# A two-stage sequence kernel: g turned by TensorE, one row layout in DRAM, fewer and larger DMAs, stores issued by ScalarE

## The chip, the cores and the metric

One core of a Trainium2 chip runs the whole program. The metric is device microseconds of one launch. The times are the median of several launches; the profile is one further launch with the hardware profiler on. TensorE is PE, VectorE is DVE, ScalarE is ACT, GpSimd is POOL and SyncE is SP. SP computes nothing here, it issues nearly all DMAs. In the rows, PEld is TensorE's weight load, and SPq and ACTq are the instruction queues of SP and ACT.

## The reference

`x` has 64 batches of 128 channels by 2048 times, in fp32. Two residual steps follow each other:

```python
x = x + einsum('bct,bcd->bdt', x, weights[condition])      # 16 possible 128x128 matrices, one is picked per batch
K = 2 * einsum('hn,hnl->hl', Ct, exp(dtA * l)).real         # one long filter of 2048 taps per channel, 64 complex modes
y = irfft(rfft(x, 4096) * rfft(K, 4096))[:2048] + x * D     # causal convolution of each channel in time, plus a gain
x = x + y * (time < length[batch])
```

The first step mixes channels inside a batch, the second works along time inside a channel. So everything has to change its layout once between them.

## The kernel before

**Mixing.** For batch n, SP loads `x_f` (128 channels by 2048 times, 1 MB). POOL makes `w_buf` (the picked matrix plus the identity), PE multiplies in four quarters of 512 columns, and the result is copied out of PSUM into `stage` with time reversed inside blocks of 128. `store_half` (L376 to L388) sends each half of a batch to DRAM in two DMAs: 48 channels to `u_wide` (192 KB, L385), 80 channels to `u_full` (320 KB, L387).

**Convolving.** It runs in 64 slots. Slots 0 to 11 are wide: four channels, batches 0 to 31. The other half of the batches of these channels comes back later as 12 more wide slots; the other 40 slots are narrow: two channels, all 64 batches. From slot 12 on the order is three narrow slots, one wide, twelve times, and then four narrow ones. A slot always handles 1 MB: `u_row`, 128 partitions of 2048 floats. `load_u` brings it as four DMAs of 256 KB in a wide slot (L395) and as two of 512 KB in a narrow one (L400), PE transposes it (L747), ACT and DVE split it into two fp16 parts in `u_t`. PE then computes the inputs to the states with `gt_sb` (L765, once per slot), advances the states over seven chunks (L781), and adds the taps (L803, L809) and the states' part (L822) to the output. ACT copies the output to `o_sb` (L942), DVE overlays the masked part (L1226), and SP stores it: `store_out`, four DMAs per slot.

**The tables.** POOL and ACT make `g_sb` for each pair of channels (called a tab; a wide slot has two, a narrow one has one). `transpose_g` turns it into `gt_sb` with two transposing DMAs per tab (L435). In slots 0 to 11 SP also keeps `g_sb` in DRAM (L439) for the later wide slots, which load it back (L419) and turn it again. The Toeplitz table comes from DRAM, one DMA of 256 KB in runs of 512 bytes per tab (L408).

**The order.** Step c of the program works on slots side by side: the taps and outputs of slot c-1, the states of slot c, the transposes of slot c+1. Each is cut into eight parts, k = 0 to 7. Batches 0 to 34 are mixed ahead of slot 0. Batches 35 to 63 are mixed in quarters inside slots 0 to 9 (`MIXED`, `LATER` = 10), with PSUM banks 6 and 7 taken in turn. SP's instructions stand in one fixed order and each waits for the one before. In a mixing slot (`mixing_slot`) SP issues 3 loads of x, 12 stores to `u_wide` and `u_full`, 4 loads of `u_row`, 2 Toeplitz loads, 4 transposing DMAs, 2 stores of g and 4 output stores: 31 DMAs. In a narrow slot it is 9. The narrow slots need both halves of the batches, so slot 12's load waits until all 64 batches have landed in DRAM.

**Two forms of output store.** In `store_out` (L442 to L455) the two kinds of slot write with different access patterns. The form of a wide slot is this, and its DRAM side begins with a dimension of four:

```python
dst = bass.AP(out.tensor, SLOTS[s].part * NBW * H * T + (SLOTS[s].first + v) * T,
              [[UNIT, 4], [H * T, NBW], [1, UNIT]])          # L447, store at L449
```

A narrow slot stores a channel in two DMAs of 64 batches by 1024 times:

```python
dst = bass.AP(out.tensor, (SLOTS[s].first + v // 2) * T + j * HALF, [[H * T, NB], [1, HALF]])   # L453, store at L454
```

Both move 256 KB each, four to a slot.

## Time and profile before

| | us |
|---|---|
| median of three launches | 1270.88 (1268.12 to 1271.56) |
| the profiled launch | 1265.78 |
| its span, first to last instruction | 1263.5 |
| PE busy | 1054.1 (83%) |
| DVE busy | 756.5 (60%) |
| POOL busy | 623.3 (49%) |
| ACT busy | 560.3 (44%) |

The launch falls into three stretches. Up to about 229 us batches 0 to 34 are mixed. Up to about 577 us slots 0 to 9 run together with the mixing of the rest. Then only slots are left. The page gives each engine's busy time over the whole, so the shares above mix three different limits. In the rows further down "DMA share" is the busy share of the 16 DMA engines in a stretch, and in the pictures of forty digits each digit is that share in tenths in a fortieth of the stretch.

### The profile page before, as it was taken

Reading aid. Unit: us, or ns where it says so; the run is one execution under the profiler, and the core shown is the slowest. Engines: PE = TensorE matmul, PEld = TensorE weight load, DVE = VectorE, ACT = ScalarE, POOL = GpSimd, SP = SyncE. Lnnn points to the kernel's source line nnn. Section 1 sums busy time; section 2 is a strip of 40 time slices with the busy share of each in tenths; the row PEclk is TensorE's granted clock in tenths of the full one; section 3 lists DMA queues with packets and bytes.
Section 4 is the critical chain, followed back from the end, with each engine's and each line's share of the span. In section 5 each row is a group of like instructions: output and inputs, shape, how many; then the busy total and the mean of one; then the engine's idle time right before and its main releaser. Section 6 shows DMA issues by size and latency. Waiting matters only on the chain.

```text
span 1263.5 us, 33041 instructions
## 1 busy us (share of the span) xinstructions
PE 1054.1 (83%) x12718; PEld 803.1 (64%) x12718; DVE 756.5 (60%) x1744; ACT 560.3 (44%) x1251; POOL 623.3 (49%) x1396
## 2 busy tenths in 40 slices
PE   8767774777767666785889999999999999999998
PEld 5223342454545444455768888888888878888886
DVE  4989710444334234333567777777777777777775
ACT  3533342333223223323345655655555555555554
POOL 3101427652344442223545757667568558657650
PEclk9988896889878878888999999999999999999999
DMA  9999999999998999998999999999899999999996
GB/s 344 393 340 398 401 353 306 264 307 271 272 264 250 265 246 254 248 245 204 167 209 258 256 210 249 254 227 249 208 272 248 214 260 256 221 249 249 199 243 155
DMA packets 238476, 330.91 MB, mean 262 GB/s; under 512 B 110242, under 2 KB 155682, under 8 KB 230130
## 3 DMA queue, kind: packets, MB, share of 16 engines
q1 hardware_dynamic: 238002, 328.35, 97.9%
q8 instruction: 103, 1.69, 0.6%
q0 software_dynamic: 160, 0.20, 0.2%
q14 instruction: 51, 0.42, 0.1%
q10 hardware_dynamic: 160, 0.26, 0.1%
HBM read 164.96 MB, written 140.71 MB: 242 GB/s over the span
## 4 chain that ended last, share of the span: by engine, by line
PE 53%; DMA 21%; SPq 19%; issue 4%; DVE 2%; ACT 2%; ACTq 0%
PE bank L803 10%; PE bank L822 10%; PE bank L765 8%; DMA u_row<-u_wide 7%; PE bank L747 7%; DMA u_row<-u_full 7%; SPq L435 6%; DMA u_full<-stage 5%; PE bank L781 5%; PE bank L713 5%; PE bank L726 4%; PE bank L809 4%; SPq L385 3%; SPq L387 2%; SPq L449 2%
## 5 line engine op out<-in xcount | busy, mean ns | idle before, releaser
L747 PE MATMUL bank<-ident,u_row 128*128 128x128 f32 x1024 | 287.0, 284 | 138.9 <-DMA u_row<-u_wide 120.2
L803 PE MATMUL bank<-toep,u_t 128*128 128x192 f16 (+1 forms) x3072 | 351.2, 223 | 0.3 <-issue 0.3
L603 POOL TENSOR_TENSOR g_sb<-g_x,g_sb 128x128 f16<-128x128 f32 x256 | 115.3, 484 | 348.5 <-ACT g_sb L891 348.5
L747 PEld LDWEIGHTS bank<-ident,u_row 128*128 128x128 f32 x1024 | 147.1, 145 | 158.9 <-DMA u_row<-u_wide 108.5
L803 PEld LDWEIGHTS bank<-toep,u_t 128*128 128x128 f16 x3072 | 237.0, 100 | 15.3 <-issue 3.9
L1204 DVE SCALAR_TENSOR_TENSOR u_t<-bank,u_t 128x512 f16<-128x512 f32 x256 | 176.3, 689 | 111.1 <-ACT u_t L920 110.0
L809 PE MATMUL bank<-toep,x_t 128*128 128x64 f16 x2048 | 193.2, 195 | 2.0 <-issue 2.0
L822 PE MATMUL bank<-g_sb,st_full 128*128 128x256 f16 x960 | 192.4, 274 | 0.2 <-issue 0.2
L920 ACT ACTIVATE u_t<-bank 128x512 f16<-128x512 f32 x256 | 151.6, 593 | 72.9 <-PE bank L747 72.3
L713 PE MATMUL bank<-x_f,w_buf 128*128 128x512 f32 x280 | 138.0, 644 | 45.6 <-issue 30.7
L765 PE MATMUL bank<-u_t,gt_sb 128*128 128x224 f16 (+1 forms) x1056 | 157.4, 302 | 9.0 <-issue 9.0
L809 PEld LDWEIGHTS bank<-toep,x_t 128*128 128x128 f16 x2048 | 161.6, 100 | 2.6 <-issue 2.2
L935 ACT ACTIVATE st_full<-bank 128x128 f16<-128x128 f32 x280 | 77.5, 277 | 174.4 <-PE bank L781 133.2
L942 ACT ACTIVATE o_sb<-bank 128x512 f32<-128x512 f32 x256 | 152.8, 597 | 4.0 <-PE bank L822 4.0
L619 POOL TENSOR_TENSOR w_buf<-w_f,ident 128x128 f32<-128x128 f32 x64 | 34.3, 538 | 222.9 <-PE bank L713 116.2
L765 PEld LDWEIGHTS bank<-u_t,gt_sb 128*128 128x128 f16 x1056 | 102.2, 98 | 54.8 <-issue 17.1
L713 PEld LDWEIGHTS bank<-x_f,w_buf 128*128 128x128 f32 x280 | 55.3, 205 | 123.1 <-issue 104.9
L726 PE MATMUL bank<-x_f,w_buf 128*128 128x512 f32 x232 | 130.9, 676 | 0.0
L1226 DVE COPY_PREDICATED o_sb<-mask,u_row 128x512 f32<-128x512 uint8 x160 | 123.5, 772 | 11.4 <-issue 11.3
L595 POOL TENSOR_TENSOR g_x<-g_x,g_y 128x128 f32<-128x128 f32 x256 | 127.3, 529 | 5.0
L610 POOL TENSOR_TENSOR lam_sb<-eyes,lam_v 128x128 f16<-128x128 f16 x256 | 118.9, 495 | 19.3 <-PE bank L781 19.3
L1209 DVE TENSOR_TENSOR st_full<-bank,st_full 128x128 f16<-128x128 f32 x280 | 81.7, 292 | 74.3 <-ACT st_full L935 71.2
(138 smaller groups left out, 1519.7 us busy)
## 6 DMA issues: line engine op xcount, KB each, us to landing
x_f<-in_x SPq DMA_DIRECT2D x64, 1024.0 KB, 10.5
out<-o_sb SPq DMA_DIRECT2D x254, 256.0 KB
u_full<-stage SPq DMA_DIRECT2D x128, 320.0 KB, 8.9
u_row<-u_full SPq DMA_DIRECT2D x80, 512.0 KB, 6.3
u_wide<-stage SPq DMA_DIRECT2D x128, 192.0 KB, 6.4
u_row<-u_wide SPq DMA_DIRECT2D x96, 256.0 KB, 8.7
toep<-k_scratch SPq DMA_DIRECT2D x88, 256.0 KB, 7.0
g_scratch<-g_sb SPq DMA_DIRECT2D x24, 256.0 KB, 4.5
```

The source lines that it names most:

```text
L595: pool.tensor_tensor(out=g_x[r][:, h, part], in0=g_x[r][:, h, part], in1=g_y[:, h, part], op=SUB)\
L713: last = pe.matmul(bank[:, 4 * (n % 2) + k, :], w_buf[n % WS][:, :], x_f[X_AT[n]][:, k * 512:(k + 1) * 512], start=True, stop=True)
L726: pe.matmul(bank[:, 6 + k % 2, :], w_buf[n % WS][:, :], x_f[X_AT[n]][:, k * 512:(k + 1) * 512], start=True, stop=True).then_inc(s_mq, 1)
L747: ins = pe.transpose(bank[:, u_bank(s, q), k % 4 * P:(k % 4 + 1) * P], ap(u_row[b], (h * groups(s) + g) * Q + tb * P, [[1, P]]), ident[:, :])
L765: last = pe.matmul(to, gt_sb[GT_AT[t]][:, hh, a, 1 - tb, :], ap(u_t[s % 3], u_at(s, h, tb, b, 0), [[1, cols]]), start=(m == 0 and fresh), ...
L803: pe.matmul(bank[:, y, col + tb * P + NM:col + Q], ap(u_t[s % 3], u_at(s, h, tb, a, gr), [[1, P]]), tp[:, hh, b, NM:Q - tb * P], start=fir ...
L809: pe.matmul(bank[:, y, col + tb * P:col + tb * P + NM], ap(x_t[s % 2], x_at(s, h, tb, gr), [[1, P]]), tp[:, hh, b, 0:NM], start=False, sto ...
L822: last = pe.matmul(bank[:, y, col:col + Q], ap(state_tile(s), st_at(s, h, a) + gr * P, [[1, P]]), g_sb[t % GS][:, hh, b, :], start=False, ...
L920: act.activation(u_t[s % 3][:, q, 0, :], bank[:, u_bank(s, q), :], ACT.Copy, scale=US).then_inc(s_uh, 1)
L942: act.activation(o_sb[o][:, v % 2, :], bank[:, 2 + v % 2, :], ACT.Copy, scale=1.0 / (US * KS))\
L1204: dve.scalar_tensor_tensor(out=t[:, q, 1, :], in0=bank[:, u_bank(s, q), :], scalar=US, in1=t[:, q, 0, :], op0=MUL, op1=SUB).then_inc(s_ul, 1)
L1226: dve.copy_predicated(o_sb[2 * (s % 2) + v // 2][:, v % 2, :].rearrange("p (b t) -> p b t", t=P), where.rearrange("p (b t) -> p b t", t=P) ...
```

## The change

It does five things.

1. `u_wide` and `u_full` become one tensor `u_dram` with 128 rows of 512 times for each channel and half of the batches. A half batch is stored in one DMA of 512 KB. Each slot loads `u_row` in two DMAs of 512 KB. All slots work with the same layout: a narrow slot is now four units of 32 batches by one channel.
2. `gt_sb` of slots 0 to 11 is made by PE: four matmuls against a swapped identity (`swap`) give half a tab in PSUM bank 6 or 7, and ACT or DVE copies it out. Mixing quarters and these halves form one list (`UNITS`); the halves of slot c+1 stand at k = 4 to 7 of step c. `g_sb` and `gt_sb` are stored in DRAM (`store_g`, two DMAs of 512 KB per slot) and the 12 later wide slots load both. The 40 narrow slots keep the transposing DMAs. A buffer of `gt_sb` can be written again only when its store has landed (`stored_g`).
3. Two Toeplitz tables that lie side by side are loaded in one DMA.
4. `store_out` uses one form for all slots, the one with the leading dimension of four. The output stores of slots 0 to 8 are issued by ACT, except for slot 8's last one; the very last slot's are shared between SP and ACT.
5. Six buffers of `x_f` are used up to batch 35 instead of 31 (`X_AT`).

The core of the diff:

```diff
-QUARTERS = {2: (1, 1, 1, 1, 1, 1, 1, 1), 3: (2, 1, 2, 1, 2, 1, 2, 1)}
+QUARTERS = {2: (1, 1, 1, 1, 1, 1, 1, 1), 3: (2, 2, 2, 2, 1, 1, 1, 1)}
-X_AT = [n % XS if n < NBW else n % (XS // 2) for n in range(NB)]
+X_AT = [n % XS if n <= FIRST else n % (XS // 2) for n in range(NB)]
...
+        def unit_copy(eng, u):
+            unit, half = UNITS[u], bank[:, 6 + u % 2, :]
+            eng.wait_ge(s_mq, u + 1)
...
+            s, last = SLOT_OF[unit.of], before(GT_AT, unit.of)
+            if last is not None:
+                eng.wait_ge(s_st, 7 * SLOT_OF[last] + 1)
+                stored_g(eng, last)
...
+        def store_out(eng, s, v):
+            o = 2 * (s % 2) + v // 2
+            eng.wait_ge(s_ov, 4 * s + v + 1)
+            dst = bass.AP(out.tensor, batches(s, v) * NBW * H * T + channel(s, v) * T, [[UNIT, 4], [H * T, NBW], [1, UNIT]])
+            eng.dma_start(dst, o_sb[o][:, v % 2, :]).then_inc(s_store[o], 16)
...
-                dst = bass.AP(u_wide, ((n // NBW * 4 + 2 * j) * NBW + n % NBW) * UNIT,
-                              [[2 * P * UNIT, H1], [NBW * UNIT, 2], [1, UNIT]])
-                sp.dma_start(dst, stage[b][0:H1, :].rearrange("p (a t) -> p a t", t=UNIT)).then_inc(s_us[b], 16)
-                dst = bass.AP(u_full, (j * NB + n) * HALF, [[P * HALF, H - H1], [1, HALF]])
-                sp.dma_start(dst, stage[b][H1:H, :]).then_inc(s_us[b], 16)
+                dst = bass.AP(u_dram, (n // NBW * P + 2 * j * NBW + n % NBW) * UNIT, [[2 * TILE, H], [NBW * UNIT, 2], [1, UNIT]])
+                sp.dma_start(dst, stage[b][:, :].rearrange("p (a t) -> p a t", t=UNIT)).then_inc(s_us[b], 16)
...
+                if last is not None:
+                    sp.wait_ge(s_ov, 4 * last + 2 * p + 2)
+                step = (channel(s, 1) - channel(s, 0)) * 2 + batches(s, 1) - batches(s, 0)
+                src = bass.AP(u_dram, (channel(s, 2 * p) * 2 + batches(s, 2 * p)) * TILE, [[UNIT, P], [step * TILE, 2], [1, UNIT]])
...
-                if n == FIRST - 2:
-                    transpose_g(0)
...
             def mixing_slot(c):
                 for k in range(8):
                     if k == 0:
                         if c > 0:
                             load_toeplitz(c)
-                        if has(c - 2):
-                            store_out(c - 2, 3)
-                        load_u(c + 1, 3)
-                    if k == 3:
-                        if c == 0:
-                            sp.wait_ge(s_kd, 80)
-                            load_toeplitz(c)
-                        transpose_g(c + 1)
-                    if k in (3, 5, 7):
-                        if has(c - 1):
-                            store_out(c - 1, k // 2 - 1)
-                        load_u(c + 2, k // 2 - 1)
+                        load_u(c + 1, 1)
+                    if k == 1:
+                        store_g(c)
+                    if k == 3 and c == 0:
+                        sp.wait_ge(s_kd, 80)
+                        load_toeplitz(c)
+                    if k == 5:
+                        load_u(c + 2, 0)
...
+                    for k in range(4):
+                        last = pe.matmul(to[:, k * P:(k + 1) * P], g_sb[of % GS][:, part, k // 2, k % 2 * P:(k % 2 + 1) * P],
+                                         swap[:, :, :].rearrange("p a m -> p (a m)"), start=True, stop=True)
...
             def out_evac(s, v):
...
+                if s < LATER - 1 and v > 0:
+                    store_out(act, s, v - 1)
+                if 0 < s < LATER - 1 and v == 0:
+                    store_out(act, s - 1, 3)
```

## Rows read from the trace of the kernel before

**Rows 1.** Busy time by stretch: engines, clock, DMA share, rate.
```profile
core 0: us, PE busy (x) PEld busy (x) DVE busy (x) ACT busy (x) POOL busy (x), PEclk, DMA share, GB/s
0.00:229.00 229.00, 163.66 (x616) 76.58 (x617) 133.76 (x327) 85.90 (x94) 70.11 (x181) 0.89 0.99 360
229.00:577.00 348.00, 249.56 (x2303) 168.15 (x2302) 133.57 (x278) 105.83 (x241) 136.82 (x348) 0.85 0.96 260
577.00:616.00 39.00, 27.22 (x434) 24.57 (x432) 19.36 (x44) 14.29 (x37) 12.42 (x29) 0.95 0.95 191
616.00:1209.00 593.00, 564.07 (x8641) 492.88 (x8640) 433.70 (x1008) 327.99 (x816) 390.05 (x812) 0.99 1.02 237
1209.00:1264.00 55.00, 49.58 (x732) 40.94 (x730) 36.08 (x89) 26.24 (x66) 13.88 (x28) 1.00 0.78 182
```

**Rows 2.** Timeline, the one L765 group of some slots: start, us, what.
```profile
229.35 2.46 PE L765 MATMUL bank<-u_t,gt_sb 128*128 128x224 f16 x24
...
287.32 2.46 PE L765 MATMUL bank<-u_t,gt_sb 128*128 128x224 f16 x24
...
576.85 1.40 PE L765 MATMUL bank<-u_t,gt_sb 128*128 128x224 f16 x8
...
615.94 2.43 PE L765 MATMUL bank<-u_t,gt_sb 128*128 128x448 f16 x12
...
631.64 2.82 PE L765 MATMUL bank<-u_t,gt_sb 128*128 128x448 f16 x12
...
709.87 1.31 PE L765 MATMUL bank<-u_t,gt_sb 128*128 128x224 f16 x12
...
721.96 2.43 PE L765 MATMUL bank<-u_t,gt_sb 128*128 128x448 f16 x12
...
1209.02 1.30 PE L765 MATMUL bank<-u_t,gt_sb 128*128 128x448 f16 x6
```

**Rows 3.** DMA packets from 100 to 150 us, in the first stretch.
```profile
DMA packets 5325, 20.07 MB, mean 401 GB/s; under 512 B 759, under 2 KB 759, under 8 KB 4083
```

**Rows 4.** DMA share and rate in forty slices, 608.5 to 612.5 us.
```profile
DMA  2239923222322222222222322322322322222329
GB/s 102 102 136 105 105 102 123 82 102 102 123 82 102 102 102 102 102 102 102 102 102 102 123 102 82 123 102 102 123 82 102 143 82 82 102 82 77 97 77 115
```

**Rows 5.** SP's queue around that, from 603 to 634 us.
```profile
603.40 1.28 SPq L400 DMA_DIRECT2D u_row<-u_full  x1
604.87 5.20 SPq L435 DMA_TRANSPOSE gt_sb<-g_sb  x2
610.12 1.62 SPq L449 DMA_DIRECT2D out<-o_sb  x2
...
617.61 1.21 SPq L400 DMA_DIRECT2D u_row<-u_full  x1
...
633.96 1.26 SPq L395 DMA_DIRECT2D u_row<-u_wide  x2
```

**Rows 6.** DMA share and rate, 626 to 630 us.
```profile
DMA  2223224302302122121234999999990000100000
GB/s 82 102 102 123 82 102 164 123 41 123 164 41 123 82 123 123 82 123 51 46 72 85 379 259 271 274 185 75 69 23 0 0 0 0 8 8 10 10 8 10
```

**Rows 7.** The same with only narrow slots' stores queued, 940 to 944 us.
```profile
DMA packets 1091, 1.38 MB, mean 344 GB/s; under 512 B 78, under 2 KB 676, under 8 KB 1090
```

**Rows 8.** Who waited for whom on PE, 229 to 577 us: total, times, longest.
```profile
PE bank L747 <- DMA u_row<-u_wide: 95.7, 25, 8.1
```

**Rows 9.** Around the first row load: SP's queue, and PE's wait.
```profile
189.72 6.95 SPq L435 DMA_TRANSPOSE gt_sb<-g_sb  x2
...
204.84 0.43 SPq L385 DMA_DIRECT2D u_wide<-stage  x1
...
217.00 1.30 PE L747 MATMUL bank<-ident,u_row 128*128 128x128 f32 x5 [17.16 <-DMA u_row<-u_wide]
```

**Rows 10.** The stores that ACT issues at the end.
```profile
1258.99 1.89 ACTq L362 DMA_DIRECT2D out<-o_sb  x2
```

More of the change, by code:

```diff
@@ L287, in stage_free @@
         def stage_free(eng, m):
-            wait(eng, s_us[STAGE_AT[m]], 32 * uses(STAGE_AT, m))
+            wait(eng, s_us[STAGE_AT[m]], 16 * uses(STAGE_AT, m))
         def stages_landed(eng, buffers, batches):
             for b in buffers:
-                eng.wait_ge(s_us[b], 32 * STAGE_AT[:2 * batches].count(b))
+                eng.wait_ge(s_us[b], 16 * STAGE_AT[:2 * batches].count(b))
         def mixing_over(eng):
-            eng.wait_ge(s_mq, 4 * (NB - FIRST))
-        def width(s):
-            return NBW if SLOTS[s].wide else NB
@@ new lines, in at, with new_state, channel, batches @@
+        def at(j):
+            return (j % 2 * 4 + j // 2) * NBW
+        def state(s, part, j):
+            return st_sb[s % 2][:, :, part, at(j):at(j) + NBW]
+        def new_state(j):
+            return ap(bank, at(j - 1), [[2 * P, 4], [1, NBW]])
+        def channel(s, v):
+            return SLOTS[s].first + (v if SLOTS[s].wide else v // 2)
+        def batches(s, v):
+            return SLOTS[s].part if SLOTS[s].wide else v % 2
+        def tab(s, v):
+            return (TABS[s][v // 2], v % 2) if SLOTS[s].wide else (TABS[s][0], v // 2)
@@ new lines, in load_toeplitz @@
+            def load_toeplitz(s):
+                t0, n = TABS[s][0], len(TABS[s])
+                together = n == 2 and TOEP_AT[t0] % 4 < 3 and TOEP_AT[t0 + 1] == TOEP_AT[t0] + 1
+                for t in [t0] if together else TABS[s]:
+                    for r in range(t, t + 1 + together):
+                        last = before(TOEP_AT, r)
+                        if last is not None:
+                            sp.wait_ge(s_out, 4 * (SLOT_OF[last] + 1))
+                    b, rows_ = TOEP_AT[t], 4 * (1 + together)
+                    src = bass.AP(k_dram, PAIR_OF[t] * (4 * KROW), [[1, P], [KROW, rows_], [1, Q]])
+                    to = ap((toep_now, toep_later)[b // 4], b % 4 * 4 * Q, [[Q, rows_], [1, Q]])
+                    sp.dma_start(to, src).then_inc(s_t[b], 16)
@@ new lines, in load_gt, with transpose_g @@
+                    sp.dma_start(gt_sb[b].rearrange("p h a b m -> p (h a b m)"), gt_dram[PAIR_OF[t], :, :]).then_inc(s_gt[b], 16)
+            def transpose_g(s):
+                t = TABS[s][0]
+                b, last = GT_AT[t], before(GT_AT, t)
+                if last is not None:
+                    sp.wait_ge(s_st, 7 * SLOT_OF[last] + 1)
+                    if SLOT_OF[last] < WIDE:
+                        stored_g(sp, last)
+                sp.sem_inc(s_go, 1)
+                sp.wait_ge(s_g, 4 * (MADE_NO[t] + 1))
+                sp.sem_inc(s_go, 1)
+                for lo in (0, NM):
+                    sp.dma_start(gt_sb[b][:, :, :, :, lo:lo + NM].rearrange("p h a b m -> p (h a b) m"),
+                                 g_sb[t % GS][NM - lo:P - lo, :, :, :].rearrange("p h a t -> p (h a t)"),
+                                 transpose=True).then_inc(s_gt[b], 16)
@@ L827, in states_part @@
                     last.then_inc(s_out, 1)
-            pe.wait_ge(s_ev, 2 * FIRST)
+            for u in range(PROLOGUE - 2):
+                unit(u)
             for k in range(8):
                 transpose_u(0, k)
-            for k in range(4):
-                mix(FIRST, k)
+            for u in range(PROLOGUE - 2, PROLOGUE):
+                unit(u)
             for k in range(8, 16):
@@ L854, in slot @@
                         between(2 * k + 1)
[L855 to L856 removed]
+                    for u in UNITS_AT[c][k]:
+                        unit(u)
                     if has(c) and k >= 2:
@@ L925, in fold_toeplitz @@
                     b = TOEP_AT[t]
-                    act.wait_ge(s_t[b], 16 * (uses(TOEP_AT, t) + 1))
+                    if landed_with(t) == t:
+                        act.wait_ge(s_t[b], 16 * (sum(landed_with(r) == r and TOEP_AT[r] == b for r in range(t)) + 1))
                     act.activation(toep[b][0:NM, :, :, 0:NM].rearrange("p h a t -> p (h a) t"),
@@ L975, in _ @@
             slots(slot)
-            for v in range(2):
-                store_last(act, 1, v)
+            for v in (1, 3):
+                store_out(act, NSL - 1, v)
         @block.vector
@@ L1224, in overlay @@
                 dve.memset(pad[0:1, at:at + 1], 0.0)
-                where = mask_w[:, SLOTS[s].part, :] if SLOTS[s].wide else mask[:, UNIT * (v % 2):UNIT * (v % 2 + 1)]
+                where = mask[:, batches(s, v), :]
                 dve.copy_predicated(o_sb[2 * (s % 2) + v // 2][:, v % 2, :].rearrange("p (b t) -> p b t", t=P),
@@ L1230, in _ @@
             make_lambda(0)
+            for u in range(1, PROLOGUE - 2, 2):
+                unit_evac(u)
             u_lo(0, 0)
             u_lo(0, 1)
-            mix_evac(FIRST, 1)
-            mix_evac(FIRST, 3)
+            unit_evac(PROLOGUE - 1)
             u_lo(0, 2)
```

431 lines of the change are left out of this document (199 added, 232 removed).

## The prediction

> **What bounds the kernel now.** I read the stretches first [rows 1], then the slots' starts [rows 2], then what PE waits for, and last SP's queue beside the DMA rate. Three stretches have three limits. Up to 229 us the DMA engines carry 360 GB/s on average and 401 in the middle of it [rows 1, 3]: that is what 16 engines give here, 25.1 GB/s each, so this stretch goes at the pace of transfers. From slot 0 to slot 10 (229.35 to 576.85, 347.5 us) PE is busy for 250 us and waits 95.7 us for `u_row` loads [rows 1, 2, 8]; transfers rule again, but at 260 GB/s. From slot 12 to slot 60 (615.94 to 1209.02, 593.1 us) PE is busy 95% of the time and sets the pace: a wide slot takes 12.09 us and a narrow one 11.35 when nothing is late [rows 1, 2], and a group of three narrow and one wide took 593.1 / 12 = 49.4 against 3 x 11.35 + 12.09 = 46.1.
>
> Why 260 GB/s when 401 is to be had? Look at the digits around 610 us [rows 4]: the share of busy engines is 2 to 3 tenths for most of 4 us and the rate stands at 102 GB/s. That is a quarter of the engines at full rate, 25.5 GB/s each. In SP's queue ahead of that stand output stores of wide slots (the L449 form), and no `u_wide` load is near [rows 5]. So I read: a store whose DRAM side begins with a dimension of four runs on four engines only, 0.262 MB / 102 GB/s = 2.57 us each. With stores of the narrow form queued the rate is 344 GB/s [rows 7], so those spread over all 16. The Trainium skill has the rule behind it (DMA: Bandwidth & Descriptors, section Why a DMA increments its semaphore by 16 and not by 1): the number of engines is the largest up to 16 that divides the slowest dimensions of both sides, here 4 and 128. By it every store of the new kernel runs on four engines, and the trace agrees for the form that it shows.
>
> **The change, the stores.** It gives the L449 form to all slots. Four stores of 256 KB then put 256 KB on each of four engines per slot, where a narrow slot's now put 64 KB on all sixteen. Work of the fullest engines in a narrow slot, in KB each: stores 256, rows 1 MB / 16 = 64, Toeplitz 16, turning 16: 352 KB. At 25.5 GB/s that is 14.1 us, more than PE's 11.35. The trace already holds this mix: from 603 to 634 us SP's cycle is one narrow slot's loads, two transposing DMAs and four wide-form stores. The two cycles took 14.21 and 16.35 us, and slot 12 to slot 13 took 15.70 on PE [rows 2, 5]. The longer one shows what is added: SP stands 5.20 us on two transposing DMAs, and at 628 us the rate falls to nothing for a moment behind the drain [rows 5, 6]. I take 15.8 us, near the two longer readings, since each narrow slot keeps its two transposing DMAs; the bounds are 14.2 and 16.4.
>
> A wide slot behind slot 12 has stores 256, rows 64, Toeplitz 32, g 32 and gt 32: 416 KB, 16.7 us, without transposing DMAs of its own; today it would be the same without its four of those. A group becomes 3 x 15.8 + 16.7 = 64.1 us, and 12 groups 769 instead of 593: +176. The bounds are 14.1 per narrow slot, giving 59.0 and +115, and 16.4 with 18.5 for the wide one (the same 10% over its bytes), giving 67.7 and +219. Behind slot 60 two slots still have loads and lose about 4 us each, and the last slot's stores need up to two more stores' time: +12 (0 to +20).
>
> **The change, the mixing slots.** Their stores have the four-engine form already. In a step with three batches the fullest engines carry 256 + (3 + 3 + 1 + 0.5 + 0.5 + 0.5) MB / 16 = 800 KB, 32.1 us, and with two batches 672 KB, 27.0. Steps 2 to 9 (slot 2 to slot 10, 289.5 us [rows 2]) hold six of the first and two of the second: 247 us, so 43 us are lost between, 5.3 per step. Each step has two pairs of transposing DMAs, and one pair held SP for 5.20 us [rows 5]. The pairs go; the extra `gt` store takes their bytes' place. I give each step 1.5 us back to other gaps: 259 us, a gain of 31, and 8 for steps 0 and 1, which lose the same pairs but hold fewer stores. Sum -39. It can't go under PE's 250 us of work plus 40 half tabs; four half tabs are 16 short matmuls per step, and I count 1 us, so the bound is -65 with some idle time left. On the other side it can be 0: 31 DMAs per step become about 19, of which four move to ACT, but SP wasn't short of time by itself, the engines were.
>
> Where new waits lie: a `u_row` pair is now loaded only after two overlays, at k = 5 instead of 3 and 5, with three eighths of a step (12 us at 32) for 512 KB to land; the copy of a half tab at k = 4 waits on ACT or DVE for the store of the half tabs of the slot before, issued at k = 1, and behind it stand the mixing copies and the states of that engine, for which PE waits. Both have about 12 us, so I price them at nothing and keep 0 as the bound above. ACT's DMA issue costs 1.89 / 2 = 0.95 us at most including gaps [rows 10]; 35 of them are 33 us of an engine that is busy 106 of 348 [rows 1]. What hides them is that slack.
>
> Here a rule speaks against me and one against the change. Advanced Engine Details and Errata, section X-Bar Transpose (TRN2), of the Trainium skill says that transposing DMAs are as fast as regular ones; then 128 KB each would be 1.3 us per step at 401 GB/s and the gain of 39 would be some 10 instead. SP's 5.20 us and the empty slices say otherwise. And DMA: Bandwidth & Descriptors, section Issuing engines are not separate DMA queues, of the skill says that a second issuing engine adds no bandwidth, only issue time; by that the move to ACT brings nothing, and I count nothing.
>
> **The change, the rest.** Ahead of slot 0 SP stands from 189.72 to 204.84 on transposing DMAs and the g stores before it issues the last row's stores and then the first row load, and PE waits 17.16 us for it until 217.00 [rows 9]. Without them that load can go about 14 us earlier; PE has batches 33 and 34 loaded earlier by the six buffers, and turns half tabs meanwhile. I take -13. Bounds -17 (all of the wait) and 0 (packets of 2 KB instead of 4 KB could cost; but the stores of [rows 4] are 2 KB packets at 25.5 GB/s per engine, no slower than the 25.1 of [rows 3]). Slots 10 and 11: their stores were of the wide form before, only the transposing pairs of slot 11 go: -3 (0 to -6). PE's narrow slots keep their columns and counts; the access patterns get one dimension more, at nothing. POOL's few memsets too.
>
> **How the numbers follow.** Against the profiled launch: 1265.8 - 13 - 39 - 3 + 176 + 12 = 1398.8. The median of the launches is 5 us (0.4%) above the profiled one, so 1404. A measurement of this kernel can tell about 0.3% (4 us) from no change.
>
> *Forecast, 57%:* 1404. Its own range is 1345 (the short cycles) to 1455.
>
> *Rival 1, the stores are hidden better, 12%.* Engines run ahead while PE waits, groups take 59.0 and the mixing goes at PE's bound: 1404 - 61 - 26 = 1317.
>
> *Rival 2, the mixing gains nothing, 12%.* The `u_row` pairs or the landed g stores are late in each step. For: two overlays and one issue instead of finer pieces. Against: 12 us each. 1404 + 39 = 1443.
>
> *Rival 3, everything in series, 9%.* SP's ring is held by the four full engines, so rows and turning can't run beside stores: 4 x 2.57 + 1.6 MB / 401 GB/s + 5.2 = 19.5 us per narrow slot, and 10.3 + 2.6 MB / 401 = 16.8 for a wide one: 75.3 per group, 904 for twelve, +135: 1539. Against it is the cycle of 14.21.
>
> *Rival 4, on the other side, 9%.* The four engines belong to something else than the form of the store (the place in the queue, the tile), and the narrow slots' stores stay spread. Then the change only removes transposing DMAs and issues, and SP's shorter wide slots let PE run at 46.1 per group: 1265.8 - 13 - 39 - 3 - 39 + 5 = 1177. The point from which it decides: a group stays at 49.4 if the fullest engine carries no more than 1229 KB, that is 195 KB per slot for stores, so from six engines on the stores cost nothing. The Trainium skill's rule for kernel authors on the same DMA page, to merge into transfers of 1 MB or more, points this way too: 256 KB stores merged into 512 KB loads.
>
> One in a hundred is left for no change, where gains and losses cancel. So faster 0.09, same 0.01, slower 0.90. The range of 1315 to 1480 leaves out rivals 3 and 4.
>
> **What the profile would show.** Right: the starts of L765 lie 15 to 17 us apart from slot 12 on; PE's busy share there falls from 95% to about 75%, with `u_row` named as what it waits for; the rate sits at about 102 GB/s with digits of 2 for long runs; slot 0 starts near 216 and slot 10 near 525. Wrong at once: a rate of 300 GB/s and intervals of 11.4 us from slot 12 on (rival 4), or slot 10 still at 560 or later (rival 2).

## The result and the profile after

| | before | after |
|---|---|---|
| median | 1271.2 us | 1371.95 us (1368.88 to 1373.14, four launches) |
| span of the profiled launch | 1263.5 | 1369.2 |
| ratio | 1 | 1.079 (1.0765 to 1.082) |

The change makes the kernel 101 us slower. The forecast was 1404, with a range of 1315 to 1480, so the sign and the range hold and the middle is 32 us too high.

The busy times by stretch, cut at the same slots as [rows 1] (slot 0, slot 10, slot 12, slot 60):

```profile
core 0: us, PE busy (x) PEld busy (x) DVE busy (x) ACT busy (x) POOL busy (x), PEclk, DMA share, GB/s
0.00:209.00 209.00, 158.45 (x633) 73.77 (x634) 132.92 (x315) 86.93 (x96) 67.45 (x167) 0.93 1.01 395
209.00:505.00 296.00, 238.42 (x2459) 165.64 (x2458) 144.72 (x297) 117.50 (x260) 133.18 (x327) 0.91 0.88 304
505.00:544.00 39.00, 28.43 (x454) 26.39 (x453) 20.19 (x47) 15.76 (x39) 18.67 (x41) 0.87 0.69 203
544.00:1292.00 748.00, 610.18 (x8640) 521.05 (x8639) 430.97 (x1009) 331.08 (x818) 355.72 (x821) 0.94 0.89 187
1292.00:1370.00 78.00, 51.49 (x730) 41.87 (x728) 35.55 (x88) 25.59 (x64) 10.53 (x24) 0.87 0.62 136
```

The starts behind these cuts, from the timeline. L793 is what L765 was in [rows 2], here at slots 0, 2, 10, 12, 13 and 60:

```profile
209.70 1.50 PE L793 MATMUL bank<-u_t,gt_sb 128*128 128x224 f16 x14
...
267.77 1.41 PE L793 MATMUL bank<-u_t,gt_sb 128*128 128x224 f16 x13
...
505.24 0.93 PE L793 MATMUL bank<-u_t,gt_sb 128*128 128x224 f16 x8
...
543.64 1.68 PE L793 MATMUL bank<-u_t,gt_sb 128*128 128x448 f16 x8
...
560.39 1.46 PE L793 MATMUL bank<-u_t,gt_sb 128*128 128x448 f16 x4
...
1291.89 1.31 PE L793 MATMUL bank<-u_t,gt_sb 128*128 128x448 f16 x6 [0.42 <-DMA gt_sb<-g_sb]
```

Subtracting the starts of [rows 2] gives the balance by stretch:

| stretch | before | after | change | forecast |
|---|---|---|---|---|
| start to slot 0 | 229.35 | 209.70 | -19.7 | -13 |
| slot 0 to 10 | 347.5 | 295.5 | -52.0 | -39 |
| slot 10 to 12 | 39.1 | 38.4 | -0.7 | -3 |
| slot 12 to 60 | 593.1 | 748.25 | +155.2 | +176 |
| slot 60 to the end | 54.5 | 77.3 | +22.8 | +12 |
| sum | | | +105.6 | +133 |

So the part up to slot 10 gains 72 us, and the slots behind slot 12 lose 178. Behind slot 12 a group of four slots takes 748.25 / 12 = 62.35 us instead of 49.4. PE does the same matmuls (8640 against 8641), but its busy share falls from 95% to 610 / 748 = 82%. What it waits for there, in order of size (total, times, longest):

```profile
PE bank L770 <- DMA u_row<-u_scratch: 112.8, 56, 4.9
PE bank L810 <- issue: 6.9, 2, 3.7
```

Of the 138 us in which PE stands, 113 are waits for rows, and the next line is 6.9.

The page's summary of the chain that ended last says the same: transfers first, then PE's own work, and SP's queue third with 6%:

```profile
DMA 49%; PE 34%; SPq 6%; DVE 4%; issue 3%; ACT 3%; DVEq 0%; ACTq 0%
```

SP's queue from 900 to 940 us shows three narrow slots. The row loads stand 14.29 and 15.36 us apart, the pair of transposing DMAs takes SP 5.4 and 6.2 us:

```profile
906.87 1.20 SPq L426 DMA_DIRECT2D u_row<-u_scratch  x1
908.27 5.39 SPq L486 DMA_TRANSPOSE gt_later<-g_sb  x2
913.71 1.88 SPq L395 DMA_DIRECT2D out<-o_sb  x2
921.16 1.54 SPq L426 DMA_DIRECT2D u_row<-u_scratch  x1
922.90 6.20 SPq L486 DMA_TRANSPOSE gt_later<-g_sb  x2
...
936.52 1.27 SPq L426 DMA_DIRECT2D u_row<-u_scratch  x1
```

Four microseconds of the DMA engines inside that, from 922 us on. In the first twelve slices two tenths of the engines work for the most part, at 82 to 159 GB/s, as in [rows 4]: stores drain. From the 21st slice on, with the next load and the transposing DMAs in flight, the rate stands between 312 and 476 for twelve slices:

```profile
DMA  4222322232223999443399899999998944798997
GB/s 159 82 82 102 143 82 82 103 123 102 82 102 123 184 225 184 143 123 102 123 405 343 312 394 476 374 333 435 471 389 328 348 156 151 195 381 207 215 184 189
```

In the mixing slots PE's wait for rows fell from the 95.7 us of [rows 8] to 50.3, and the new wait for the stored half tabs appears four times on DVE:

```profile
PE bank L770 <- DMA u_row<-u_scratch: 50.3, 14, 8.6
...
DVE gt_sb L1220 <- DMA gt_scratch<-gt_sb: 17.2, 4, 6.5
```

At the end the last compute instruction stops at 1351.0 us and 18 us follow in which only stores run. From 1356 to 1369 us they stay at 101 GB/s, with digits of 2, until they run out in the last four slices:

```profile
1350.28 0.72 DVE L1255 COPY_PREDICATED o_sb<-mask,u_row 128x512 f32<-128x512 uint8 x1 [0.70 <-issue]
...
DMA  2222222222222222222222222222222222221000
GB/s 101 101 101 101 101 101 101 113 88 113 101 101 101 101 101 113 101 101 101 101 101 101 101 101 101 101 101 113 101 101 101 101 101 101 101 113 69 19 0 0
```

### The profile page after: what moved, and what is told of

The parts are those of the page before. It is cut to its first block, busy times and chain, and to the rows that moved or that the text cites. A ratio compares the mean times of both kernels' runs of the same rounds, so it can differ in the third digit from the quotient of the medians.

```text
span 1369.2 us, 33160 instructions
## 1 busy us (share of the span) xinstructions
PE 1087.0 (79%) x12910; PEld 828.7 (61%) x12910; DVE 764.3 (56%) x1754; ACT 576.9 (42%) x1275; POOL 585.5 (43%) x1377
## 4 chain that ended last, share of the span: by engine, by line
DMA 49%; PE 34%; SPq 6%; DVE 4%; issue 3%; ACT 3%; DVEq 0%; ACTq 0%
DMA u_row<-u_scratch 33%; DMA u_scratch<-stage 9%; PE bank L831 6%; PE bank L849 6%; PE bank L770 5%; PE bank L748 5%; PE bank L793 4%; DMA gt_scratch<-gt_sb 4%; PE bank L736 3%; PE bank L837 2%; PE bank L810 2%; SPq L395 2%; DVE o_sb L1255 2%; DVE u_t L1233 2%; SPq L462 2%
## 5 line engine op out<-in xcount | busy, mean ns | idle before, releaser
L849 PE MATMUL bank<-g_sb,st_sb 128*128 128x256 f16 x1536 | 326.6, 286 | 4.6 <-issue 4.6
L961 ACT ACTIVATE st_sb<-bank 128x128 f16<-128x128 f32 x448 | 123.9, 277 | 310.1 <-PE bank L810 220.7
L1238 DVE TENSOR_TENSOR st_sb<-bank,st_sb 128x128 f16<-128x128 f32 x448 | 130.2, 291 | 173.6 <-ACT st_sb L961 167.8
L831 PE MATMUL bank<-toep,u_t 128*128 128x192 f16 (+1 forms) x1752 | 208.2, 226 | 0.0
L1255 DVE COPY_PREDICATED o_sb<-mask,u_row 128x512 f32<-128x512 uint8 x256 | 195.9, 766 | 16.0 <-issue 15.9
L849 PEld LDWEIGHTS bank<-g_sb,st_sb 128*128 128x128 f16 x1536 | 155.7, 102 | 13.1 <-issue 4.8
L831 PE MATMUL bank<-toep_later,u_t 128*128 128x192 f16 (+1 forms) x1320 | 154.8, 226 | 2.6 <-issue 2.6
L810 PE MATMUL bank<-st_sb,lam_sb 128*128 128x32 f16 (+1 forms) x3168 | 147.0, 184 | 9.4 <-issue 6.9
L810 PEld LDWEIGHTS bank<-st_sb,lam_sb 128*128 128x128 f16 x3168 | 132.3, 97 | 35.7 <-issue 21.3
L831 PEld LDWEIGHTS bank<-toep,u_t 128*128 128x128 f16 x1752 | 139.5, 103 | 11.3 <-issue 3.9
```

Of the source, the lines that this page charges most:

```text
L810: last = pe.matmul(ap(bank, v * 2 * P + at(j), [[2 * P, n], [1, NBW]]), lam_sb[t % LS][:, h, a, :, :].rearrange("p k m -> p (k m)"), st_sb ...
L831: pe.matmul(bank[:, y, col + tb * P + NM:col + Q], ap(u_t[s % 3], v * 2 * UNIT + a * UNIT + tb * 2 * P + gr * P, [[1, P]]), tp[:, h, b, NM ...
L849: last = pe.matmul(bank[:, y, col:col + Q], st_sb[s % 2][:, v, a, gr * P:(gr + 1) * P], g_sb[t % GS][:, h, b, :], start=False, stop=(m == ...
L1238: dve.tensor_tensor(out=state(s, 1, j), in0=new_state(j), in1=state(s, 0, j), op=SUB).then_inc(s_stl, 1)
L1255: dve.copy_predicated(o_sb[2 * (s % 2) + v // 2][:, v % 2, :].rearrange("p (b t) -> p b t", t=P), where.rearrange("p (b t) -> p b t", t=P) ...
```

## The experiments

The theory is that the store with a leading dimension of four runs on four engines, and that this alone makes the loss. The main rivals are that the stores aren't the cause (rival 4), that their addresses are and not the number of engines, that SP's queue is (transposing DMAs, order), and that the move to ACT matters.

### The number of engines: sixteen, eight, and sixteen for narrow slots only

`k16_all` and `k8_all` keep the number and size of all stores and their place in the program. They change only the addresses in `out`, so that the leading dimension is 16 or 8; the output lands in another order, so these kernels serve for timing alone. `k16_narrow` does it for narrow slots alone.

```diff
-            dst = bass.AP(out.tensor, batches(s, v) * NBW * H * T + channel(s, v) * T, [[UNIT, 4], [H * T, NBW], [1, UNIT]])
+            k = 16                  # k8_all: 8; k16_narrow: 4 if SLOTS[s].wide else 16
+            row = 4 * NSL * UNIT
+            dst = bass.AP(out.tensor, (4 * s + v) * UNIT, [[row, k], [k * row, P // k], [1, UNIT]])
```

> The changed kernel with one edit: the DRAM side of each output store begins with a dimension of 16 instead of 4; same 256 KB, same runs of 2 KB, same waits. The output lands in another order, so it isn't the reference's. Theory (stores of the old form fill four engines, and these set the pace): from slot 12 on PE sets the pace again, a group of three narrow slots and a wide one takes 46 to 48 us instead of 62.4 (-180), the mixing steps fall from 296 to about 265, the end shrinks by 20: 1372 - 180 - 30 - 20 = about 1140, and no run of slices at 102 GB/s is left. Rival (the loss comes from the pair loads of u_row, from runs of 2 KB or from the new waits, not from the stores): 1372, unchanged.

> As k16_all, but the store's leading dimension is 8. Theory: the fullest engines carry 4 x 128 + 448 = 960 KB per group, 38.6 us, which is under PE's 46.1, so the time is within 20 us of k16_all (1140 to 1160): the number of engines costs nothing above the point where PE sets the pace. Rival (the cost goes with the share of engines left idle): half way between 1140 and 1372, about 1255.

> As k16_all, but only for narrow slots; the 24 wide slots keep a leading dimension of 4. Theory: the mixing steps stay at 296 us, groups take about 48 us, so 1372 - 173 - 20 = about 1180, which is what the fourth rival of the prediction gave (1177). If wide slots behind slot 12 slow their neighbours too, up to 1200. Rival (not the stores): 1372.

Measured, with the ratio to the kernel before:

| | us | ratio | slot 0 to 10 | group behind slot 12 |
|---|---|---|---|---|
| changed kernel | 1372.0 | 1.079 (1.0765 to 1.082) | 295.5 | 62.4 |
| `k16_all` | 1112.7 | 0.876 (0.869 to 0.883) | 253.7 | 46.5 |
| `k8_all` | 1132.9 | 0.891 (0.884 to 0.898) | 261.7 | 47.5 |
| `k16_narrow` | 1177.1 | 0.925 (0.918 to 0.932) | 294.6 | 48.3 |

The two stretches of `k16_all`, slot 0 to 10 and slot 12 to 60, then slot 12 to 60 of `k8_all`:

```profile
209.50:463.20 253.70, 230.65 (x2459) 161.28 (x2458) 146.34 (x297) 116.39 (x259) 137.21 (x326) 0.95 1.01 355
498.40:1056.90 558.50, 555.61 (x8642) 490.20 (x8641) 432.44 (x1009) 327.65 (x817) 397.22 (x816) 1.00 0.97 252
```

```profile
506.30:1076.00 569.70, 558.04 (x8642) 491.45 (x8641) 432.44 (x1009) 327.90 (x817) 393.07 (x816) 1.00 1.01 247
```

The same number of stores of the same size, issued at the same places, cost 259 us less. PE is busy for 555.6 of 558.5 us: it sets the pace again, with next to nothing late. Eight engines are nearly as good as sixteen, about as the break-even of rival 4 has it (from six engines on the stores cost nothing in a group). They are not quite free: the intervals of the two ratios don't overlap, and a group takes 1.0 us more. `k16_narrow` makes rival 4's condition true, and its 1177.1 stands beside the 1177 that was worked out for that rival. The agreement of the totals hides terms that were off and cancelled, as said further down.

The number of engines shows in the last 4 us of these launches too, where stores are all that is left. With a leading dimension of four the rate was 101 GB/s and the digits 2 (above). With eight (`k8_all`, 1128.4 to 1132.4 us) the commonest rate is 205, with digits around 5:

```profile
DMA  6454556355545735391465445543310000000000
GB/s 225 164 205 164 205 205 205 123 205 225 205 164 225 205 123 164 123 205 61 164 246 184 164 164 225 205 164 123 143 41 20 0 0 0 0 0 0 0 0 0
```

With sixteen (`k16_all`, 1106.7 to 1110.7 us) the digits are mostly 8 and 9, and the rate comes up to some 400, in one slice to 492:

```profile
DMA  0035969498979999889999987988632000000000
GB/s 0 0 82 164 225 123 287 82 205 225 328 287 369 410 389 287 287 348 492 369 389 369 369 205 205 287 307 307 246 143 82 0 0 0 0 0 0 0 0 0
```

### The same form in the kernel before

Is the form also what held the kernel before in its mixing slots? `before_k16` is the kernel before with only the stores of wide slots at a leading dimension of 16. They go to another tensor, so that part of the output, 96 of the 256 stores (not half, as the expectation has it), is missing.

```diff
-                    dst = bass.AP(out.tensor, SLOTS[s].part * NBW * H * T + (SLOTS[s].first + v) * T,
-                                  [[UNIT, 4], [H * T, NBW], [1, UNIT]])
+                    row = 4 * NSL * UNIT
+                    dst = bass.AP(spill, (4 * s + v) * UNIT, [[row, 16], [16 * row, P // 16], [1, UNIT]])
```

> The kernel before with one edit: the stores of its 24 wide slots (96 of 256) go with a leading dimension of 16 to another DRAM tensor, so half of the output is missing. Theory: slots 0 to 9 were held by four engines as well; 348 us become about 300, slots 10 to 15 lose some 25 us of waits, later groups 1 us each: about 1190. Rival (in the mixing slots of before SP's issues and transposing DMAs were the limit, not the four engines): the mixing stays near 340 and only slots 10 to 15 gain, 1240.

Measured 1180.35 us, 0.929 (0.921 to 0.937). Slot 0 to 10 took 290.8 us instead of 347.5, a group 47.5 instead of 49.4:

```profile
230.80:521.60 290.80, 233.65 (x2301) 158.83 (x2300) 134.08 (x277) 105.47 (x241) 141.02 (x345) 0.91 1.04 310
```

So the kernel before carried the same fault in 24 of its 64 slots, for 89 us (1269.45 in this comparison). Its mixing slots took 290.8 with the transposing DMAs and everything else as it was.

### A form that leaves the output where it is: each store cut by time

`split4` stores what a pair of 256 KB stores held in four DMAs of 128 KB, one for each quarter of the time. Each has 32 partitions on the SBUF side and a leading dimension of 32 batches on the DRAM side.

```diff
+            if v % 2 == 0:
+                return
...
-            dst = bass.AP(out.tensor, batches(s, v) * NBW * H * T + channel(s, v) * T, [[UNIT, 4], [H * T, NBW], [1, UNIT]])
-            eng.dma_start(dst, o_sb[o][:, v % 2, :]).then_inc(s_store[o], 16)
+            first = batches(s, v - 1) * NBW * H * T + channel(s, v - 1) * T
+            step = batches(s, v) * NBW * H * T + channel(s, v) * T - first
+            for a in range(4):
+                dst = bass.AP(out.tensor, first + a * UNIT, [[H * T, NBW], [step, 2], [1, UNIT]])
+                eng.dma_start(dst, o_sb[o][a * NBW:(a + 1) * NBW, :, :]).then_inc(s_store[o], 16)
...
```

> The changed kernel, complete, in its own row order; only each pair of output stores of 256 KB becomes four stores of 128 KB, one per time quarter, 32 partitions each. Their DRAM side then begins with 32. The price is four DMA issues more per slot (13 instead of 9 in a narrow one, 0.6 us each: 8.0 + 2.4 = 10.4 us of SP in 11.35 of PE). Theory (four engines): near k16_all, 1115 to 1145, faster than both kernels. Rival (the permuted addresses of k16_all were easier on DRAM, or SP becomes the bound): 1200 or more, with PE waiting for row loads.

Measured 1128.49 us (1127.1 to 1134.7), 0.885 (0.881 to 0.889). That is faster than both kernels: 243 us under the changed one and 145 under the one before. Slot 0 to 10, slot 12 to 60, and the issues of the stores on SP (ns shortest/median/longest):

```profile
209.50:463.10 253.60, 228.43 (x2460) 160.21 (x2459) 149.10 (x297) 115.86 (x260) 137.65 (x327) 0.95 1.00 355
498.70:1071.40 572.70, 559.12 (x8643) 491.43 (x8642) 435.90 (x1009) 328.55 (x818) 392.87 (x816) 1.00 0.98 246
```

```profile
L400 SPq DMA_DIRECT2D out<-o_sb x440: 315/432/2440, 463.4 to 1121.5; - x147
```

There are twice as many store DMAs of half the size, and the median issue takes SP 432 ns. A group takes 47.7 us, close to the 47.5 of `k8_all` and 1.2 us over the 46.5 of `k16_all`; whether the issues cost that difference isn't shown.

`before_split4` makes the same cut in the wide stores of the kernel before, and nothing else:

```diff
+                    if v % 2 == 0:
+                        return
...
-                    dst = bass.AP(out.tensor, SLOTS[s].part * NBW * H * T + (SLOTS[s].first + v) * T,
-                                  [[UNIT, 4], [H * T, NBW], [1, UNIT]])
-                    sp.dma_start(dst, o_sb[o][:, v % 2, :]).then_inc(s_store[o], 16)
+                    for a in range(4):
+                        dst = bass.AP(out.tensor, SLOTS[s].part * NBW * H * T + (SLOTS[s].first + v - 1) * T + a * UNIT,
+                                      [[H * T, NBW], [T, 2], [1, UNIT]])
+                        sp.dma_start(dst, o_sb[o][a * NBW:(a + 1) * NBW, :, :]).then_inc(s_store[o], 16)
...
```

> The kernel before, complete, in which only the output stores of its 24 wide slots are cut: each pair of 256 KB becomes four of 128 KB whose DRAM side begins with 32. It asks how much of the kernel before was held by four engines, with the true addresses. Theory: like before_k16, 1175 to 1200, though SP gets four issues more in steps where it already had 31 (0.45 us each, so up to 15 us more in the mixing steps). Rival (SP's issues were the limit of the mixing steps): 1240 or more.

Measured 1174.68 us, 0.922 (0.9185 to 0.9255):

```profile
229.60:520.80 291.20, 239.18 (x2302) 160.78 (x2301) 134.33 (x277) 104.91 (x241) 137.55 (x336) 0.90 1.04 307
```

Now the change can be taken apart. The kernel before is at 1273.6 in this comparison; spreading its wide stores gives 1174.7 (-99), all the rest of the change on top of that gives 1128.5 (-46), and the four-engine form on every store puts 243 back. Of the 46, 38 lie between slot 0 and 10 (291.2 to 253.6) and 20 ahead of slot 0 (229.60 to 209.50); behind slot 12 it gives back 11 (562.0 to 572.7).

### The move to ACT

`sp_stores` gives the stores of slots 0 to 8 back to SP, at the places that they had before.

```diff
+                        if has(c - 2):
+                            store_out(sp, c - 2, 3)
...
+                    if k in (3, 5, 7) and has(c - 1):
+                        store_out(sp, c - 1, k // 2 - 1)
...
-                if s < LATER - 1 and v > 0:
-                    store_out(act, s, v - 1)
-                if 0 < s < LATER - 1 and v == 0:
-                    store_out(act, s - 1, 3)
```

> The changed kernel with the output stores of slots 0 to 8 issued by SP, as in the kernel before; form with the leading dimension of 4 kept. The prediction counted nothing for the move to ScalarE: 1372, within 10 us. Rival: stores that fill four engines hold up SP's queue and everything behind it, which ACT's own queue avoids: the mixing steps go from 296 back towards 330, so 1390 to 1410.

Measured 1379.5 us, 1.083 (1.076 to 1.091), against the changed kernel's 1.079 (1.0765 to 1.082). The intervals overlap, so this run can't tell the two apart. Its profile has 303.0 us between slot 0 and 10 against 295.5, and one store issue that held SP for 6.7 us:

```profile
L395 SPq DMA_DIRECT2D out<-o_sb x36: 542/554/6696, 245.2 to 512.0; - x36
```

A gain of up to some 8 us from ACT is therefore possible beside four-engine stores, and not shown. The same step in a kernel with spread stores is `batch_major_sp`, below.

### The turning in the narrow slots

`no_turn` is the changed kernel whose narrow slots load the same number of bytes into `gt_sb` in two plain DMAs instead of two transposing ones. They come from DRAM and are the table of another pair, so the narrow slots leave out the turning and don't give the reference's result.

```diff
+                stored_g(sp, 0)
...
-                    sp.dma_start(gt_sb[b][:, :, :, :, lo:lo + NM].rearrange("p h a b m -> p (h a b) m"),
-                                 g_sb[t % GS][NM - lo:P - lo, :, :, :].rearrange("p h a t -> p (h a t)"),
-                                 transpose=True).then_inc(s_gt[b], 16)
+                    sp.dma_start(gt_sb[b][lo:lo + NM, :, :, :, :].rearrange("p h a b m -> p (h a b m)"),
+                                 gt_dram[0, lo:lo + NM, :]).then_inc(s_gt[b], 16)
```

> The changed kernel, but the 40 narrow slots load gt with two plain DMAs of 128 KB from the table of pair 0 instead of turning their own g, so their numbers are wrong. It tests the part of the sum that was put on turning, 1.7 us per narrow slot over the bytes of the fullest engines. Theory: groups fall from 62.4 to about 59 us, 1372 - 41 = 1331. Rival (the fullest engines work without a gap anyway): groups stay at 62, 1372.

Measured 1348.6 us, 1.057 (1.051 to 1.063), where 1331 was expected. Slot 12 to 60:

```profile
551.40:1275.00 723.60, 604.69 (x8642) 517.96 (x8641) 433.46 (x1009) 330.94 (x817) 357.51 (x819) 0.94 0.57 193
```

A group takes 723.6 / 12 = 60.3 us, 2.05 less than the 62.35 of the changed kernel: 0.7 us per narrow slot. The profiled launch is the slowest of the four, 5 us over the median, which is at most 0.14 us more per narrow slot. The forecast put 1.7. And 60.3 is close to the 59.0 that the bytes of the fullest engines alone give.

### The other way to spread the stores: rows in another order

`batch_major` puts the batch ahead of the quarter in the order of the 128 rows. A store then has a leading dimension of 32, stays one DMA of 256 KB and writes the very addresses that the changed kernel's store writes; only the order of the dimensions differs. The states of one chunk stand four elements apart in `st_sb` and in PSUM.

```diff
-            return (j % 2 * 4 + j // 2) * NBW
+            return j % 2 * P + j // 2
...
-            return st_sb[s % 2][:, :, part, at(j):at(j) + NBW]
+            return ap(st_sb[s % 2], part * 2 * P + at(j), [[4 * P, 4], [4, NBW]])
...
-            dst = bass.AP(out.tensor, batches(s, v) * NBW * H * T + channel(s, v) * T, [[UNIT, 4], [H * T, NBW], [1, UNIT]])
+            dst = bass.AP(out.tensor, batches(s, v) * NBW * H * T + channel(s, v) * T, [[H * T, NBW], [UNIT, 4], [1, UNIT]])
```

> The changed kernel, complete, with the rows of a tile ordered by batch first and time quarter second. The DRAM side of an output store then begins with a dimension of 32, and the half batches are stored in runs of 4 KB. The price is 32 idle columns more in each L765 matmul (about 0.3 us per slot, 20 us in all) and state copies with a step of four. Theory (four engines): 1113 + 20 = about 1130, faster than both kernels. Rival (the permuted addresses of k16_all were easier on DRAM than the true ones with their pitch of 1 MB): 1200 or more.

Measured 1261.4 us, 0.991 (0.987 to 0.994): 111 us under the changed kernel, and some 130 over what was expected. Slot 0 to 10 took 250.5, which is as good as `k16_all`. With the same addresses, number and size of stores as in the changed kernel, which took 295.5, this leaves the order of the dimensions and speaks against the addresses as the cause (the half batches are stored in runs of 4 KB here instead of 2 KB). But a group took 58.0 us, with PE's busy time at 660 us where `k16_all` has 556, and its clock at 1.00:

```profile
496.10:1192.00 695.90, 659.70 (x8643) 521.70 (x8642) 483.54 (x1008) 381.29 (x815) 370.12 (x814) 1.00 0.72 201
```

The groups by line show what grew. Busy us and mean ns of the two copies of a state, in the changed kernel first:

```profile
L961 ACT ACTIVATE st_sb<-bank 128x128 f16<-128x128 f32 x448 | 123.9, 277 | 310.1 <-PE bank L810 220.7 <-PE bank L793 89.4
L1238 DVE TENSOR_TENSOR st_sb<-bank,st_sb 128x128 f16<-128x128 f32 x448 | 130.2, 291 | 173.6 <-ACT st_sb L961 167.8
```

```profile
L959 ACT ACTIVATE st_sb<-bank 128x128 f16<-128x128 f32 x448 | 207.6, 463 | 363.8 <-PE bank L808 278.9 <-PE bank L791 84.6
L1236 DVE TENSOR_TENSOR st_sb<-bank,st_sb 128x128 f16<-128x128 f32 x448 | 199.8, 446 | 253.5 <-ACT st_sb L959 253.5
```

The seven chunks are a chain of PE, ACT, DVE, and two of its links grew by 186 and 155 ns. The timeline of `batch_major` shows this chain closed, each link starting within 0.15 us of the end of the one before:

```profile
804.39 0.52 PE L808 MATMUL bank<-st_sb,lam_sb 128*128 128x64 f16 x6
...
804.95 0.46 ACT L959 ACTIVATE st_sb<-bank 128x128 f16<-128x128 f32 x1 [1.18 <-PE bank L808]
...
805.45 0.45 DVE L1236 TENSOR_TENSOR st_sb<-bank,st_sb 128x128 f16<-128x128 f32 x1 [0.48 <-ACT st_sb L959]
...
806.04 0.52 PE L808 MATMUL bank<-st_sb,lam_sb 128*128 128x64 f16 x6
```

A chunk takes 1.65 us here and 1.18 in `k16_all`, where PE is busy for 555.6 of 558.5 us. The two copies alone are 7 x 0.341 = 2.4 us per slot, 115 us in 48 slots, of the 137 by which the stretch is longer than in `k16_all` (695.9 against 558.5). So the chain sets the pace here, although PE is busy 95% of the time. What differs in the copies is the step of four elements in their access patterns.

`batch_major_sp` is `batch_major` with the stores of slots 0 to 8 on SP, the edit of `sp_stores`.

> batch_major with the output stores of slots 0 to 8 issued by SP at k = 0, 3, 5, 7 of the step, as in the kernel before. Theory (a second issuing engine brings nothing where the DMA engines or PE set the pace): within 10 us of batch_major. Rival (SP, which stands in one order, delays row loads while it waits for overlays): 15 to 30 us slower.

Measured 1260.1 us, 0.989 (0.985 to 0.992), beside 0.991 (0.987 to 0.994) with ACT. Where the stores are spread, the move to ACT brings nothing that can be measured.

`batch_major2` asks which side makes the copies slow. It keeps the columns in PSUM side by side, and has the step of four in SBUF alone: `st_sb` is written with it, and L792 reads `u_t` with it, one unit at a time.

```diff
-            return ap(bank, at(j - 1), [[2 * P, 4], [4, NBW]])
+            return ap(bank, (j - 1) * NBW, [[2 * P, 4], [1, NBW]])
...
-                                         ap(u_t[s % 3], v * 2 * UNIT + b * UNIT + tb * 2 * P, [[2 * UNIT, n], [1, cols]]),
+                                         ap(u_t[s % 3], w * 2 * UNIT + b * UNIT + tb * 2 * P, [[1, 4], [P, 2], [4, NBW]]),
```

> batch_major, complete, with the states' columns in PSUM in a row again; the step of four stays on the SBUF side (st_sb written, u_t read in L791). In batch_major the state copies went from 277 and 291 ns to 463 and 446. If the step in PSUM made them slow, they are back under 320 ns and the time is about 1150; if the step in SBUF did, they stay over 400 ns and the time stays near 1260.

Measured 1428.4 us, 1.119 (1.113 to 1.126), which is neither of the two expected times. But the question has its answer: with PSUM contiguous the copy on ACT takes 464 ns, as in `batch_major`. So the step in SBUF is enough to make it slow. The extra time is in L792, which reads `u_t` at the same step: its 1536 matmuls are busy for 360 us, where the 1056 of L791 in `batch_major` were for 178. L792 also writes PSUM in blocks of 32 columns in another order, which no run separates from the read. That covers the 167 us between the two runs. The copy, then one of the groups of L792:

```profile
L960 ACT ACTIVATE st_sb<-bank 128x128 f16<-128x128 f32 x448 | 207.9, 464 | 545.0 <-PE bank L809 279.0 <-PE bank L792 265.9
L792 PE MATMUL bank<-u_t,gt_sb 128*128 128x256 f16 x912 | 213.5, 405 | 0.0
```

In `batch_major` the matmul over 256 contiguous columns took 273 ns:

```profile
L791 PE MATMUL bank<-u_t,gt_sb 128*128 128x256 f16 x432 | 50.6, 273 | 0.0
```

## Why the prediction was right, and where its sizes were off

**What bounds a slot behind slot 12: right.** The step from the digits of [rows 4] to "a leading dimension of four means four engines" carried the sign, and it holds: `k16_all` and `k8_all` change that dimension and the addresses, `batch_major` changes it and keeps the addresses, and in all three the loss at the stores is gone. That it was read from 4 us of the trace of before was a risk: in those 4 us 88 of the 258 packets are under 512 bytes, so the stores weren't alone. The narrow form in the same trace at 344 GB/s [rows 7] spoke for the reading, and the end of the changed kernel, with stores alone at 101 GB/s, bears it out. PE's pace was right as well: 46.1 us for a group with nothing late, and `k16_all` takes 46.5.

**12 groups, +176 forecast, +155 measured.** The byte sum (14.1 per narrow slot, 16.7 for the wide one) gives 59.0 per group, and without transposing DMAs the group takes 60.3. The step that was mis-sized is the one from 14.1 to 15.8 us, the price of turning. I took it from the two longer of three readings; `no_turn` has it at 0.7 us instead of 1.7. That is 3 us per group too much, and the byte sum's 1.3 us too little; together they are the 64.1 - 62.35 = 1.75 us per group, 21 us in twelve.

**PE's share, forecast 75%, measured 82%.** PE's busy time in the stretch grew from 564 to 610 us though it did the same matmuls, beside a granted clock of 0.94 instead of 0.99. With 564 / 748 the share would have been 75%. The forecast took busy time as fixed.

**Mixing slots, -39 forecast, -52 measured.** Two sizes were off, in opposite directions. Steps 0 and 1, for which I put a gain of 8, gained nothing: 58.1 us (209.70 to 267.77) against 58.0 before. Steps 2 to 9, for which I put 31, gained 52. They took 237.5 us (267.77 to 505.24), which is less than the 247 that I took for the bytes alone at 25.5 GB/s, and I had added 1.5 us per step. From 100 to 150 us the changed kernel moves 416 GB/s, where the kernel before had 401 [rows 3]:

```profile
100.00:150.00 50.00, 37.06 (x142) 15.46 (x141) 44.00 (x109) 19.76 (x20) 10.90 (x24) 1.00 1.03 416
```

That is 26 per engine, and at this rate 5 of the 9.5 us are accounted for. Where the rest of them is isn't settled. The doubt that the Trainium skill raised (Advanced Engine Details and Errata, section X-Bar Transpose (TRN2): transposing DMAs as fast as regular ones, hence a gain of some 10) is answered by halves. For the narrow slots the runs come close to what it says, since a plain pair in place of a transposing one saves only 0.7 us. For the mixing slots `before_split4` to `split4` shows 38 us gained with all stores spread. But turned tabs, fewer DMAs and one layout all go together there, and the share of each wasn't measured.

**Ahead of slot 0, -13 forecast, -20 measured.** That is beyond the bound of -17, which took the wait of 17.16 us [rows 9] as all there was to win. The whole first stretch also moves faster, 395 GB/s against 360, and this term was missing. The first row load is issued 23 us earlier, where I put 14; the load of the kernel before comes behind the stores that start at 204.84 in [rows 9]. Before, then after:

```profile
209.00 3.04 SPq L395 DMA_DIRECT2D u_row<-u_wide  x4
```

```profile
185.74 1.17 SPq L426 DMA_DIRECT2D u_row<-u_scratch  x2
```

**The end, +12 forecast, +23 measured.** The step "up to two more stores' time" failed. At the rate of four engines the stores still waiting when the last compute ends are 18 / 2.57 = 7, nearly the whole of two slots, since they had piled up behind each other.

**The new waits, priced at nothing.** DVE did wait for the landing of half tabs, 17.2 us in four times, and the mixing slots gained all the same. The wait for both overlays ahead of a row pair doesn't show: the wait for rows is smaller than before.

**The move to ACT, counted at nothing: right within what can be told.** The Trainium skill says (DMA: Bandwidth & Descriptors, section Issuing engines are not separate DMA queues) that DMAs run on the same 16 engines whichever engine issues them, and that a second issuer saves issue time only. `batch_major_sp` agrees, 0.989 against 0.991.

**The rivals.** Rival 1 gave 1317, because it took the short cycles and PE's bound in the mixing; the mixing did go lower than forecast, but the groups stand at 62.4 and not 59.0. Rival 2 fell with slot 10 at 505 instead of 560. Rival 3 fell since a narrow slot takes 15, not 19.5. Rival 4 fell on its condition. That `k16_narrow` took just its 1177 is in part luck: the groups took 48.3 us and not 46.1, which gains 14 us instead of 39, and the mixing slots (294.6, a gain of 53 instead of 39) and the stretch ahead of slot 0 (209.5, a gain of 20 instead of 13) made up for most of it. The remark beside it on merging doesn't touch the output stores: they stay at 256 KB, and what the change merges are loads and the stores of half batches.

**The sum.** For the profiled launch the forecast was 1398.8 and the time 1370.96, 28 us less; the other 4 come from the median. I put it 5 us above the profiled launch, as before. After the change it stands 1371.95 - 1370.96 = 1.0 above. By stretches the gain ahead of slot 12 was 17 us more and the groups' loss 21 us less than forecast, and the loss at the end, 11 us more, took part of that back, so the total is a little nearer than its terms.

What stays open: `k16_all` is 16 us under `split4`, which may be the count of DMAs or the addresses, and no run separates them.

## What to carry to other kernels

Before you change how a DMA is shaped, look at the slices of DMA share and rate while only that DMA is in flight: a steady quarter of the full rate meant here that a quarter of the engines worked, and a group of slots took about what the bytes of these fullest engines take (60.3 us against 59.0 without transposing DMAs). Cut such a transfer so that its leading dimension is larger (8, 16 and 32 all did it here), even if that makes twice as many DMAs of half the size: 1372 became 1128 us here. And when an edit bundles several steps, try the suspected one alone on the kernel before: its own worst part was already there, for 99 us.

## What was unexpected of the hardware

- Eight engines were nearly enough: 1132.9 us against 1112.7 with sixteen, where four gave 1372.
- A step of four fp16 elements in SBUF isn't free: a copy of 128x128 from PSUM went from 277 to 463 ns on ACT, its counterpart on DVE from 291 to 446, and a matmul over 256 columns of such an operand took 405 ns against 273 with the columns side by side.
- The DMA share isn't a measure of how near the engines are to their limit. Slot 12 to 60 had a share of 0.89 at 187 GB/s with transposing DMAs and 0.57 at 193 GB/s without, for a difference of 2 us in 62; and it was 0.97 at 252 GB/s in `k16_all`, in which PE waited for next to nothing.
